# A fused token-mixing and ternary-MLP layer: the first tile's back half reordered, the last tile given its own order of products

## The reference, cut to what matters

```python
# 1. token mixing
h  = layernorm(x)
hp = h shifted by one token
k, v, r = mix(h, hp, tmk) @ Wk.T, mix(h, hp, tmv) @ Wv.T, sigmoid(mix(h, hp, tmr) @ Wr.T)
wkv = running, numerically stable recurrence over tokens (state p: running max, state q: numerator)
x  = x + (r * wkv) @ Wo.T
# 2. MLP with ternary weights (-1, 0, 1) and a scale for each output
h  = layernorm(x)
h  = silu((h @ w1.T) * s1) * ((h @ w2.T) * s2)        # 256 -> 1024
h  = gelu((h @ h1.T) * sh1)                           # 1024 -> 1024
h  = gelu((h @ h2.T) * sh2)                           # 1024 -> 1024
x  = x + (h @ w3.T) * s3                              # 1024 -> 256
```

## Time and profile before

| | us |
|---|---|
| median of three runs | 1498.48 (1498.16 to 1498.81) |
| profiled execution, its own time | 1496.86 |
| its span in the trace | 1495.2 |
| TensorE busy in the span | 1477.4 |
| VectorE, ScalarE, GpSimd busy | 1220.9, 1078.1, 263.3 |
| mean granted clock, share of full | 0.998 |

### The profile page before, as it was taken

One profiled execution on the slowest core, in us unless ns is written; L12 is line 12 of the kernel. 1 busy time (PEld: TensorE's weight loads), 2 busy tenths in 40 slices (PEclk: granted clock), 3 DMA queues, 4 the chain that ended last, 5 costly groups with the idle time before them and its releaser, 6 DMA issues.

```text
span 1495.2 us, 28878 instructions
## 1 busy us (share of the span) xinstructions
PE 1477.4 (99%) x10334; PEld 1326.6 (89%) x10334; DVE 1220.9 (82%) x1627; ACT 1078.1 (72%) x1626; POOL 263.3 (18%) x526
## 2 busy tenths in 40 slices
PE   8999999999999999999999999999999999999998
PEld 6879899898989989899898988989899898998998
DVE  7897987878878787887878978788887879878664
ACT  6886686867768677686866868677587776868664
POOL 2204012040211203112030120302112031120300
PEclk9999999999999999999999999999999999999999
DMA  9958374664646557374673645656464663746553
GB/s 347 383 217 302 108 253 117 205 197 142 231 118 226 153 181 240 98 242 119 204 220 123 231 136 203 178 166 230 101 237 135 202 226 105 252 115 206 171 190 121
DMA packets 94910, 285.28 MB, mean 191 GB/s; under 512 B 9120, under 2 KB 33312, under 8 KB 92960
## 3 DMA queue, kind: packets, MB, share of 16 engines
q1 hardware_dynamic: 86720, 277.01, 54.5%
q0 software_dynamic: 8160, 7.87, 4.3%
HBM read 250.76 MB, written 33.03 MB: 190 GB/s over the span
## 4 chain that ended last, share of the span: by engine, by line
PE 95%; DVE 3%; POOL 1%; DMA 1%; ACT 1%; issue 0%; SPq 0%; DVEq 0%; POOLq 0%; ACTq 0%
PE acc L640 26%; PE acc L642 26%; PE att L549 10%; PE acc L614 7%; PE acc L615 7%; PE acc L666 4%; PE acc L668 4%; PE att L572 3%; PE att L528 2%; PE att L615 1%; PE att L614 1%; PE acc L759 1%; PE acc L761 1%; DMA stage<-in_w_ffn 1%; PE acc L525 1%
## 5 line engine op out<-in xcount | busy, mean ns | idle before, releaser
L640 PE MATMUL acc<-op_hi,ring 128*128 128x256 f32 x3360 | 810.9, 286 | 1.4 <-DVE parts L1663 1.4
L642 PE MATMUL acc<-op_lo,ring 128*128 128x256 f32 x3360 | 788.9, 278 | 0.0
L640 PEld LDWEIGHTS acc<-op_hi,ring 128*128 128x128 f32 x3360 | 632.0, 188 | 19.8 <-issue 18.7
L642 PEld LDWEIGHTS acc<-op_lo,ring 128*128 128x128 f32 x3360 | 631.2, 188 | 11.1 <-issue 10.0
L1601 DVE TENSOR_TENSOR op_lo<-blocks,op_hi 128x1024 fp32r<-128x1024 f32 (+2 forms) x271 | 340.9, 1272 | 91.0 <-ACT op_hi L1008 85.5
L1008 ACT ACTIVATE op_hi<-blocks 128x1024 fp32r<-128x1024 f32 (+2 forms) x263 | 283.8, 1091 | 80.9 <-DVE blocks L1596 76.2
L2025 POOL TENSOR_TENSOR v_sb<-mix_v,v_sb 128x1024 f32<-128x1024 f32 (+1 forms) x19 | 39.5, 2081 | 801.9 <-DVE r_sb L1530 786.2
L614 PE MATMUL acc<-x_hi,w_rnd 128*128 128x512 f32 x420 | 167.4, 399 | 0.9 <-issue 0.9
L615 PE MATMUL acc<-x_lo,w_rnd 128*128 128x512 f32 x420 | 166.2, 396 | 0.0
L1048 ACT ACTIVATE blocks<-acc,vec 128x256 f32<-128x256 f32 x268 | 105.2, 476 | 63.4 <-PE acc L642 62.6
L1048 ACT ACTIVATE blocks<-parts,vec 128x256 f32<-128x256 f32 x240 | 102.3, 497 | 57.4 <-DVE parts L1658 49.5
(11 more groups left out here) (183 smaller groups left out, 2186.4 us busy)
## 6 DMA issues: line engine op xcount, KB each, us to landing
ring<-scratch SPq DMA_DIRECT2D x427, 512.0 KB, 4.1
scratch<-stage SPq DMA_DIRECT2D x11, 1024.0 KB, 10.7
stage<-in_w_ffn SPq DMA_DIRECT2D x10, 1024.0 KB, 10.8
x_in<-in_x SPq DMA_DIRECT2D x32, 256.0 KB, 4.5
out<-x_next SPq DMA_DIRECT2D x30, 256.0 KB, 4.8
out<-mix_v POOLq DMA_DIRECT2D x30, 256.0 KB, 4.4
scratch<-in_w_ffn SPq DMA_DIRECT2D x4, 1024.0 KB, 11.8
ring<-stage SPq DMA_DIRECT2D x7, 512.0 KB, 9.2
```

Source lines behind the costliest of these rows:

```text
L640: pe.matmul(out, act(w), act(op_hi[:, k, c, :]), start=(begins and c == 0 and m % 2 == 0), stop=False, skip_group_check=True)
L642: mm = pe.matmul(out, act(w), act(op_lo[:, k, c, :]), start=False, stop=(c == QC - 1), skip_group_check=True)
```

## The change

It touches four places.

- **Start of tile 0.** For the early sequence VectorE's running max reads k from PSUM (`first_running_max`), and ScalarE's copies of k wait for it. The copies of v and r stand behind two exponentials.
- **Middle and back of tile 0.** SP does all seven refills, then the loads of two areas, then the two stores. TensorE sums flags 3 before `project` of chunks 4 and 5, and flags 4 at the start of `first_last`. ScalarE does all checks of ring halves before the copies of v, `gelu_plain(0, 1, 1)` between these copies, and the sum checks in another order. VectorE sets flag 3 between its clamps, and does a low part and a block sum behind the recurrence. POOL does `hi_plain(0, 1, 1)` before `numerator`.
- **Last tile's order.** For `l` = 0 TensorE takes `LAST_OPERANDS`, and SP fills the ring by `LAST_WEIGHTS`. Waits that look up a step's place go by the same table (`operands(i)`). The lists of ScalarE and VectorE for these steps are not changed.
- **The end.** Token blocks 0 and 1 go to banks of their own, and are finished and stored one by one.

```diff
+        LAST_OPERANDS = [(B11, T1, T2, B21, T3, B22, T4), OPERANDS[1]]
+        LAST_WEIGHTS = [(A11, S1, S2, A12, S3, S4, A22), WEIGHTS[1]]
+        def operands(t):
+            return LAST_OPERANDS if isinstance(t, int) and t == NT - 1 else OPERANDS
+        LAST_BLOCK = BANK[6][:, 0:D]
...
-            refill_plain(0, range(4))
-            store_sum(0, 2)
-            refill_plain(0, range(4, 5))
-            store_sum(0, 3)
-            refill_plain(0, range(5, SLOTS))
+            refill_plain(0, range(SLOTS))
             sp.wait_ge(low_done, 9)
+            sp.wait_ge(sums[0], 3)
             sp.wait_ge(st_sum[0][0], 16)
             load_area(1, A22_)
             sp.wait_ge(st_sum[0][1], 16)
             load_area(1, A21_)
+            store_sum(0, 2)
+            store_sum(0, 3)
             sp.wait_ge(low_done, DONE[3] + 1)
...
-                    k = OPERANDS[l][s]
+                    k = operands(i)[l][s]
...
+                    if between is None:
+                        accumulate(0, B11, 0, True, LAST_BLOCK)
+                        accumulate(1, B11, 0, True)
+                        pe.wait_ge(dve_loG21.sem, dve_loG21.at(i))
+                        accumulate(0, B21, QC, False, LAST_BLOCK).then_inc(pe_block, 1)
+                        accumulate(1, B21, QC, False).then_inc(pe_block, 1)
+                        return
...
                 def first_last():
+                    pe.wait_ge(act_g12.sem, act_g12.at(0, 2 * QC))
+                    sum_flags(4)
                     pe.wait_ge(act_g22.sem, act_g22.at(0, QC))
...
                     accumulate(3, T1, 0, False)
-                    sum_flags(4)
...
-                    project(WHOLE, 1, [2, 3, 4])
+                    project(WHOLE, 1, [2, 3])
                     sum_flags(3)
-                    project(WHOLE, 1, [5])
+                    project(WHOLE, 1, [4, 5])
...
+                    if s is FIRST[0] and which == 0:
+                        act.wait_ge(first_scan, e + 1)
...
-            copy_kvr(early_seq, 0, [2, 3])
             exp(early_seq, 0, 0)
             exp(early_seq, 0, 1)
-            copy_kvr(early_seq, 0, [4, 5])
+            copy_kvr(early_seq, 0, range(2, 3 * DC))
...
-            for n in range(1, 6):
+            for n in range(1, SLOTS):
                 check_half(n)
+            assert checked[0] == DONE[3]
             copy_kvr(WHOLE, 1, [2])
-            check_half(6)
-            assert checked[0] == DONE[3]
+            gelu_plain(0, 1, 1)
             copy_kvr(WHOLE, 1, [3])
...
-            gelu_plain(0, 1, 1)
-            gelu_plain(1, 0, 0)
             check_sum(0, 2)
             check_sum(0, 3)
+            gelu_plain(1, 0, 0)
             check_sum(1, 0)
             gelu_plain(1, 1, 0)
             check_sum(1, 1)
-            check_sum(1, 2)
             gelu_plain(1, 0, 1)
             copy_x1(WHOLE, 1)
+            check_sum(1, 2)
             check_sum(1, 3)
...
+            def first_running_max(s):
+                dve.wait_ge(s.dve_mix.sem, s.dve_mix.at(0))
+                dve.wait_ge(s.act_x.sem, s.act_x.at(0))
+                link(s, dve.tensor_copy(seq[:, :, s.seqs, 0:1], carry_p[:, :, s.seqs]))
+                settle(s, 0)
+                n = s.pairs[0]
+                for c in range(DC):
+                    dve.wait_ge(s.pe_kvr.sem, s.pe_kvr.at(0, c + 1))
+                    dve.tensor_tensor_scan(
+                        now[:, c, n, :], decay[:, c:c + 1].broadcast_to([P, SEG]), s.banks[KVR_BANK[c]][:, s.cols],
+                        carry_p[:, c, n, :], ALU.add, ALU.max).then_inc(first_scan, 1)
+                dve.wait_ge(first_scan, DC)
+                link(s, dve.tensor_copy(carry_p[:, :, s.seqs], seq[:, :, s.seqs, SEG:SEG + 1]))
+                dve.wait_ge(s.act_kvr.sem, s.act_kvr.at(0, DC))
...
-            def finish_last(k, j):
+            def finish_last():
...
+                for b, bank in enumerate((LAST_BLOCK, Z[:, D:2 * D])):
+                    dve.wait_ge(pe_block, b + 1)
+                    dve.tensor_tensor(out_tok[:, b, :], bank, s3_row[:], ALU.mult).then_inc(dve_last, 1)
+                    dve.wait_ge(dve_last, 2 * b + 3)
+                    dve.tensor_tensor(out_tok[:, b, :], out_tok[:, b, :], x1_next[:, b, :], ALU.add).then_inc(dve_last, 1)
...
-            first_exponents(WHOLE, 1)
+            next_exponents(WHOLE, 1)
+            settle(WHOLE, 1)
+            next_clamps(WHOLE, 1, 0)
             set_flag(3)
+            now_exponents(WHOLE, 1)
+            settle(WHOLE, 1)
+            now_clamps(WHOLE, 1, 2)
             lo_plain(T1, dve_loT1, 3)
-            block_sum(1, 0)
             gain(WHOLE, 1)
             recurrence(WHOLE, 1, 0)
             recurrence(WHOLE, 1, 1)
+            lo_plain(B22, dve_loB22, 4)
+            block_sum(1, 0)
             denominator(WHOLE, 1)
...
             lo_plain(T1, dve_loG12, 7)
+            set_flag(4)
             lo_plain(B22, dve_loG22, 8)
             finish(0, 1, 0)
             rest_x2(WHOLE, 1)
-            set_flag(4)
...
-            finish_last(1, 1)
-            finish_last(2, 0)
+            finish_last()
...
             hi_plain(0, 0, 1)
+            hi_plain(0, 1, 1)
             numerator(WHOLE, 1)
-            hi_plain(0, 1, 1)
```

More of the change, by code:

```diff
@@ L1777, in _ @@
                 mix(early_seq, 0, which)
-            for c in range(DC):
-                running_max(early_seq, 0, c)
+            first_running_max(early_seq)
             first_exponents(early_seq, 0)
@@ L1862, in _ @@
             weigh(WHOLE, 1)
-            lo_plain(B22, dve_loB22, 4)
             block_sum(1, 1)
```

50 lines of the change are left out of this document (27 added, 23 removed).

## The result

| | before | after |
|---|---|---|
| median of the runs made side by side | 1498.16 us (1497.39 to 1498.81, 9 runs) | 1501.37 us (1498.85 to 1504.7, 9 runs) |
| ratio, 95% interval | | 1.0021 (1.0012 to 1.003) |
| profiled execution, its own time | 1496.86 us | 1499.08 us |
| its span | 1495.2 us | 1497.3 us |

The change makes the kernel slower, by 3.2 us where the forecast had 6.4. The runs of the changed kernel also scatter over 5.9 us, those of before over 1.4. A ratio here compares the runs of a kernel with those of before and comes with a 95% interval; turned into microseconds it can differ from the difference of two medians, and the text says which of the two it gives.

The account below looks back on a forecast made before the run. TensorE, busy 1477.4 of 1495.2 us, was taken as the bound. Start +0.2, middle and back -2.5, last tile +6.7, clock +2.6 and tail -0.6 sum to +6.4 us: 1504.9 from the 1498.48 median, range 1501.0 to 1508.2.

Parts of the forecast that it names:

- 6.7 us net: Last tile: stalls before T3 and T4 make T4 start at 1458.8 instead of 1452.08, the old 1.41 us wait already off.
- The clock's term: Last tile: TensorE's clock falls after the 5.6 us stall and perhaps after the 2.5 us one, +2.6 us.
- the middle, "-1.8 us": First tile: refills ahead of stores shorten the 1.92 us wait; next block starts at 101.7 instead of 103.50, -1.8 us.
- The second wait of 0.4 us: First tile, middle: TensorE idles 0.4 us more for the other copy of v, which stands behind four gelus.
- the 0.5 us put down for the branch: First tile, middle: an estimated 0.5 us from the products' end at 101.2 to the next block at 101.7.
- the 0.85 us before the loop: End of first tile: the wait at the branch, given as 0.9 us, shrinks by half with the earlier flag, -0.4 us.
- The -0.3 for the low part: First tile, back: the cast moved ahead on POOL removes TensorE's 0.34 us wait before 123.12, -0.3 us.
- The start of tile 0: Scans read PSUM and the second copy follows them; net cost +0.2 us, bounds -0.6 and +0.5.
- the middle doesn't do what it says: Rival, first tile: fills land as late as now, a second wait costs 1.6 us; total +9.4, 1507.9 us; chance 0.12.
- stall without the clock, and with all the gains: Rival: the last tile stalls, the clock costs nothing, other gains come in full; +2.4, 1500.9 us; chance 0.06.
- VectorE's -0.5: Tail: finishing blocks singly leaves a multiply and add on 128x256 after the last matmul, not 128x512, -0.5 us.
- The store's "-0.1": Tail: the last store is 128 KB instead of 256, saving 0.1 us, up to 0.2.

Follow-up runs that it names:

- e2: The changed kernel with matmuls on a free bank put before T3 (six) and T4 (two) in the last tile: 1498.06 us, ratio 1.0008.
- e4: The kernel before with only the last tile's order of products and weights changed: 1507.22 us, ratio 1.006.
- e10: The changed kernel with the last tile's order and the tail undone, leaving the first tile's edits alone: 1493.79 us, ratio 0.9972.
- e14: e9 run once more, beside the kernel before on the same chip: 1489.4 us, ratio 0.9948.
- e13: e9 with the old tail, the last pair finished whole and stored as one DMA of 256 KB: 1491.72 us, ratio 0.9958.
- e5: The kernel before with the change's tail alone: 1496.66 us, ratio 0.9991.
- e6: e1 with SP's two stores of summed blocks put back between the ring's fills: 1495.02 us, ratio 0.9981.
- e7: e1 with the last flags summed and set right before the branch into the loop again: 1494.71 us, ratio 0.9981.
- e8: The kernel before with the last pair's 256 KB stored as two DMAs of 128 KB: 1497.28 us, ratio 0.9998.
- e15: e9 with the last two blocks still finished one by one but stored as one DMA of 256 KB: 1490.0 us, ratio 0.9954.
- e16: e13 with its last 256 KB store cut into two DMAs of 128 KB, issued at the old moment: 1491.28 us, ratio 0.9966.
- e3: The changed kernel with ScalarE's and VectorE's lists of the last tile put into the new order of products: 1490.45 us, ratio 0.9953.
- e1: The changed kernel with the last tile's order of products and weights as before: 1490.88 us, ratio 0.9953.
- e12: The changed kernel with SP waiting for the refill's last half before it issues the area's loads: 1499.04 us, ratio 1.0022.
- e9: e3 with SP waiting for the refill's last half to land before it issues the 1 MB area loads: 1489.62 us, ratio 0.9952.

## Why the prediction was right and wrong

**Right: which way, and why.** The orders of ScalarE and VectorE were left behind, T3 waited 5.61 us for u2 and T4 2.54 us for c22. The prediction had 5.6 and 2.5, and 6.7 us net. The clock's term of 2.6 us measured 2.2 to 2.3 in the profiles (after against before and against e2); in e4, where it fell twice, it was 1353.1 - 1348.7 = 4.4. Order and clock alone gave +9.0 (e4) against 9.3. The time, 1501.37, lay near the lower end of the range of 1501.0 to 1508.2, and outside the forecast's own 1501.8 to 1507.5.

**Wrong: the size, by two gains that were both put too small.**

| term | forecast | in the two profiles | runs, by the ratios |
|---|---|---|---|
| first tile (start, middle, back, branch) | -2.3 | -4.3 | -4.2 (e10) |
| last tile, waits and clock | +9.3 | +8.9 | +9.0 (e4) |
| tail | -0.6 | -2.4 | -1.5 (e14 against e13), -1.3 (e5) |
| sum | +6.4 | +2.2 | +3.3 with -1.5; the change +3.1 |

The column of the two profiles compares one execution with one. The seventeen profiled executions, cut at the loop's first matmul and at the last matmul, show how much each part swings (us; e6 and e7, whose first tiles are mixed, began the loop at 148.39 and 147.84, and e8, e15 and e16, whose ends are mixed, are not in the last row):

| stretch | as before | as changed |
|---|---|---|
| start to the loop | 147.67, 148.50, 148.50, 148.85 (before, e4, e8, e5) | 143.36, 143.64, 144.61, 146.88, 147.06 (after, e2, e3, e1, e10); 143.20 to 144.46 with SP's wait (six) |
| loop to the last matmul | 1342.0 to 1342.2 (seven) | 1351.0, 1350.6 (after, e12); 1353.1 (e4, two falls of the clock); 1348.7 (e2, none); 1340.8 to 1341.0 with the lists (six) |
| last matmul to the end | 5.4 to 5.5 (before, e10, e13); 4.9 (e4) | 3.0 to 3.2 (seven), 4.5 to 4.8 (e5, e6, e7) |

Swings of 3.7, 2.1 and 1.7 us in the three parts can make a scatter of 5.9 us.

*The first tile.* The step that failed is the middle, "-1.8 us", which measured 103.50 - 100.16 = -3.3 in the two profiled executions, with -4.2 for the whole first tile by e10's ratio. Its working lost 1.5 us at three places. The product behind the wait was put at 97.4 and came at 96.83: the check began at 95.05, where the fill's landing was put at 95.35, and its readout and the copy overlap. The second wait of 0.4 us for the copy behind the gelus did not occur: the copy, at 98.00, was done before TensorE got there. And the 0.5 us put down for the branch between the products and the next block was nothing: TensorE shows no gap there, with the flag set before. Nor was there anything left of the 0.85 us before the loop, of which the prediction had taken off only half; the change takes it away whole, and e7 brings 1.08 back. For both branches an estimate without a row stood in the sum. The -0.3 for the low part came (3.3 us at 100.16, 3.6 at 134.25). The start of tile 0, +0.2 in the sum, was -0.1: the next step began at 15.68, not 15.77.

The rival *the middle doesn't do what it says* was wrong on the mean and half right in single executions. In e1, e7 and e10, with the area's loads in flight, the check of the last half began only at 97.4 to 98.2 us, and the clock fell; in e1 and e10 the loop still began 0.6 to 0.8 us earlier than before. That scatter was in no case of the forecast. The rival *stall without the clock, and with all the gains* had 1500.9, the number nearest to the measured one, but by luck: the clock did fall, and the gains were larger than its own.

*The tail.* VectorE's -0.5 held: from the last matmul to the end of the last add 1491.20 - 1489.75 = 1.45 us passed before and 1495.23 - 1494.32 = 0.91 after. The store's "-0.1" failed: it was 1.9 us between e13 and e14, and again between the two profiles. The step took the 3.7 us for a price of 256 KB and scaled it by size, with a load into the ring as the second point. It is mostly no price of size, but that of a share of the store that waits for another queue's packet at that moment; where the packet comes early, the changed tail pays it too (e5, e6, e7). The Trainium skill (DMA: Bandwidth & Descriptors, "Anatomy of one DMA") gives 2.0 us plus bytes over 436 GB/s for a DMA issued by GpSimd, not for every DMA as the prediction has it. Carried over to these stores, which SP issues, it makes an estimate of 2.6 us for 256 KB and 2.3 for 128 KB. Undisturbed stores here took 2.2 and 1.7 us, below that fit, and the disturbed one 3.6 us. The prediction saw the 1.1 us between the row and the fit and took the row, but did not ask what the difference was.

The errors have one sign. By the ratios they are 1.9 us in the first tile, 0.9 in the tail and 0.3 in the last tile. Taken off the forecast of +6.4 they leave +3.3, against +3.1 measured.

## What to carry to other kernels

When the order of one engine's products changes, write out the lists of every engine that fills or empties its buffers: the new order was harmless in itself (e3), and cost 10 us with the old lists. A transfer on which TensorE waits should not only be issued first; in some executions it was still late with large loads right behind it, and in none of six when they were held until it had landed, at no cost in the median (e9, e14). Before a duration is scaled by size, look at its slices in the DMA view: here a long thin tail was a share held up by another queue's packet, and it vanished in most executions when the transfer started half a microsecond earlier. And cut more than one profiled execution at the same instructions before a difference of two is called a gain: the first tile's swung by 3.7 us.

## What the runs showed of the hardware that was not expected

- The instruction queue (q8) moves packets of 16 KB, which took 0.9 to 1.7 us each near the end of the runs. A sixteenth of a store can come behind one, and the store then lands 1.4 us later (e13 3.6 us, e15 2.2 us, both 256 KB) or 1.5 to 1.8 us later (e5, e6 and e7 against the other seven, 128 KB).
- Fills of 512 KB with 2 MB of loads issued right behind them began to be checked between 95.05 and 98.15 us in six executions, with the loads held back between 94.86 and 96.13. The three latest (from 97.40) also brought a fall of the clock of 3.4 us. A fall need not follow a wait at once: in e5 and e8, whose first tile is that of before, TensorE waited 1.7 and 1.9 us for the copy of v at the same place, the clock stayed at 2.4 GHz there and fell at 124 us, behind a wait of 2.0 and 1.9 us for a low part.
- Two scans that read PSUM take 1.39 us, the same as two that read SBUF before (14.27 us, 1.39 us), and the next step starts within 0.1 us of where it did:

```profile
13.78 1.39 DVE L1481 TENSOR_TENSOR_SCAN seq<-vec,carry_p,acc 128x256 f32<-128x256 f32 x2
```
